# Attention scores on TensorE: base rows of two heads on different halves of the partitions

## What is computed

```python
q, k, v = heads(x @ Wq.T), heads(x @ Wk.T), heads(x @ Wv.T)      # 16 heads of 16
scores = einsum('bhid,bhjd->bhij', q, k) / sqrt(hd)
std_out = out_proj(softmax(where(mask, scores, neg)))            # plain
qg, qd = splat_feats(q)                                          # exp(-distance), tanh(direction)
kg, kd = splat_feats(k)
splat_attn = einsum('bhin,bhjn->bhij', amp * qg, kg) \
    + directional_strength * einsum('bhin,bhjn->bhij', amp * qg * qd, kg * kd)
gsa_out = out_proj(softmax(where(mask, scores + position_sensitivity * splat_attn, neg)))   # guided
attn = (1.0 - blend) * std_out + blend * gsa_out
x = layernorm(x + attn)
h = silu(x @ w_gate) * (x @ w_up)
x = layernorm(x + keep_2_largest_of_4(h) @ w_down)
```

## Time and profile before

| | us |
|---|---|
| median of 3 runs | 396.21 |
| lowest, highest run | 395.86, 396.52 |
| span of the profiled execution | 396.0 |
| PE busy in it | 372.8 (94%) |
| DVE busy | 303.9 (77%) |
| ACT busy | 229.6 (58%) |
| POOL busy | 125.7 (32%) |

### The profile page before, as it was taken

How to read it: one execution, slowest core, us unless ns; L and a number is a source line. 1 busy time by engine, 2 the same in 40 slices (tenths; PEclk the granted TensorE clock), 3 DMA queues, 4 the chain that set the end, 5 groups by cost and what they waited for, 6 DMA issues and landing times.

```text
span 396.0 us, 6714 instructions
## 1 busy us (share of the span) xinstructions
PE 372.8 (94%) x2234; PEld 255.1 (64%) x2234; DVE 303.9 (77%) x900; ACT 229.6 (58%) x451; POOL 125.7 (32%) x173
## 2 busy tenths in 40 slices
PE   6998999999999999999999999999889899999995
PEld 6666568565665665675664664764435488888884
DVE  2766999997897897897898898795024367999955
ACT  3965443675675685684784774775766836443100
POOL 8377657403303303302302312284395200000000
PEclk9998999999999999999999999999989999999999
DMA  6062540450540540540550558000000000000003
GB/s 201 22 105 47 81 81 4 67 95 10 88 70 4 87 75 6 89 73 4 82 82 3 80 86 319 4 2 0 5 0 2 0 2 0 0 2 0 2 0 106
DMA packets 12907, 19.70 MB, mean 50 GB/s; under 512 B 5492, under 2 KB 8564, under 8 KB 12872
## 3 DMA queue, kind: packets, MB, share of 16 engines
q1 hardware_dynamic: 10328, 18.18, 22.9%
q0 software_dynamic: 1536, 1.07, 1.6%
q10 hardware_dynamic: 1008, 0.02, 0.1%
HBM read 5.26 MB, written 1.05 MB: 16 GB/s over the span
## 4 chain that ended last, share of the span: by engine, by line
PE 69%; DVE 19%; ACT 6%; issue 2%; DMA 2%; SPq 1%; POOL 0%; DVEq 0%; ACTq 0%
PE ps L937 17%; PE ps L963 14%; PE ps L902 13%; DVE ps L1270 11%; PE ps L863 7%; PE ps L765 5%; PE ps L767 5%; PE ps L766 5%; DVE mpart L1263 2%; PE ps L924 2%; ACT pr L713 2%; DMA x_sb<-_attn_hidden_states_dram 2%; DVE mpart L1270 2%; PE ps L847 1%; PE ps L827 1%
## 5 line engine op out<-in xcount | busy, mean ns | idle before, releaser
L713 ACT ACTIVATE pr<-ps 128x512 f32<-128x512 f32 (+2 forms) x320 | 154.8, 571 | 75.8 <-PE ps L963 74.7
L1270 DVE CUSTOM_DVE_ANT_0 ps<-ps,causal 128x512 f32<-128x512 f32 (+3 forms) x256 | 144.9, 615 | 19.0 <-PE ps L902 18.2
L902 PE MATMUL ps<-k_st,q_st 65*128 65x512 f32 (+5 forms) x384 | 120.9, 369 | 3.5 <-DVE mpart L1270 2.8
L963 PE MATMUL ps<-q_st,k_st 67*128 67x512 f32 (+7 forms) x384 | 122.2, 363 | 0.3 <-ACT pr L713 0.3
L963 PEld LDWEIGHTS ps<-q_st,k_st 67*128 67x128 f32 (+1 forms) x384 | 68.3, 191 | 39.4 <-issue 21.5
L902 PEld LDWEIGHTS ps<-k_st,q_st 115*128 115x128 f32 (+1 forms) x384 | 67.9, 190 | 25.8 <-DVE mpart L1270 15.7
L937 PE MATMUL ps<-pr,vx 128*32 128x512 f32 (+3 forms) x768 | 74.1, 497 | 1.9 <-ACT o_sb L699 1.0
L558 POOL TENSOR_SCALAR_AFFINE_SELECT pr<-pr 128x512 f32<-128x512 f32 x64 | 40.5, 634 | 87.7 <-ACT pr L713 87.3
L1263 DVE TENSOR_REDUCE mpart<-ps 128x1 f32<-128x384 f32 (+2 forms) x96 | 54.9, 596 | 7.3 <-PE ps L902 7.0
L937 PEld LDWEIGHTS ps<-pr,vx 128*32 128x32 f32 x768 | 19.4, 109 | 32.1 <-issue 17.4
L1270 DVE DVE_READ_ACCUMULATOR2_ANT mpart<- 128x1 f32 x256 | 36.0, 141 | 0.0
(11 more groups left out here) (190 smaller groups left out, 497.5 us busy)
## 6 DMA issues: line engine op xcount, KB each, us to landing
q_st<-base_hiq SPq DMA_DIRECT2D x28, 64.0 KB
k_st<-base_hik SPq DMA_DIRECT2D x28, 64.0 KB
q_st<-feat_hiq SPq DMA_DIRECT2D x28, 64.0 KB
k_st<-feat_hik SPq DMA_DIRECT2D x28, 64.0 KB
x_sb<-_attn_hidden_states_dram SPq DMA_DIRECT2D x4, 256.0 KB, 6.5
raw<-in_L_ffn_w_gate_dram SPq DMA_DIRECT2D x1, 1024.0 KB, 4.8
raw<-in_L_ffn_w_up_dram SPq DMA_DIRECT2D x1, 1024.0 KB, 7.0
wd<-in_L_ffn_w_down_dram SPq DMA_DIRECT2D x1, 1024.0 KB, 9.1
```

Source lines behind the costliest of these rows:

```text
L713: act.activation(pr[:, s % NP, 2 * hh + vs[0]:2 * hh + vs[-1] + 1, d:BANK], src, ACT.Exp, scale=SCALE).then_inc(exp_done, 1)
L902: mm = pe.matmul(ps[:, slot, at:at + n], q_st[b][0:rows, hh, i * P:(i + 1) * P], k_st[b][0:rows, hh, first:first + n], start=(v == v0), st ...
L963: mm = pe.matmul(ps[:, bank, j * width:(j + 1) * width], k_st[b][0:rows, hh, kt * P:(kt + 1) * P], q_st[b][0:rows, hh, q:q + width], start ...
L1270: ins = dve.tensor_tensor_reduce(out=ps[:, slot, at:at + n], in0=ps[:, slot, at:at + n], in1=causal[:, BANK - n:BANK], scale=1.0, scalar=- ...
```

## The change

Head 0 keeps its base rows on partitions 0 to 47 and puts its feature rows on 64 to 111. Head 1 has them the other way round: features on 0 to 47, base on 64 to 111. In each half two rows behind them hold maxima. So the plain matmuls of head 0 use partitions 0 to 63 and those of head 1 use 64 to 127, 64 rows each, and the guided ones of both use all 128. k's stack is all ones before its rows are filled, q's all zeros.

The plain matmuls of the two heads stand one behind the other: `score_parts` has the heads innermost, `row_items` too from pair 1 on, and `leads` marks a maxima item whose partner of head 1 is taken with it. Nothing is put between the first two parts of a wide step. `rows` on DVE makes three operations of two, since each half of the partitions has its own order of plain and difference, and SP clears two pairs of rows instead of one when a buffer is used again.

```diff
-    BASE, FEAT = 0, 67
-    M_ROW, D_ROW = 65, FEAT + 3 * SPL
-    ZERO = 3 * HD
-    PLAIN, GUIDED = M_ROW, D_ROW
+    HROWS = P // KC
+    M_OFF = 3 * HD
+    Z_OFF = M_OFF + 2
+    BOTH = slice(0, P)
+    def own_rows(hh):
+        return slice(HROWS * hh, HROWS * hh + HROWS)
+    def base_row(hh):
+        return HROWS * hh
+    def feat_row(hh):
+        return HROWS * (1 - hh)
...
-        return [(hh, v, d, w) for hh in range(2) for v in ([(0, 1)] if w <= HALF else [(0,), (1,)])]
+        return [(hh, v, d, w) for v in ([(0, 1)] if w <= HALF else [(0,), (1,)]) for hh in range(2)]
...
+        return [("max", p, hh, i, c, v, nv) for i in range(T)
+                for c, piece in enumerate(row_pieces(i)) for v, nv in banks(piece) for hh in range(KC)]
+    def leads(it):
+        return it[0] == "max" and it[1] > 0 and it[2] == 0 and it[5:] == (0, 1)
...
+            for _ in range(2 if leads(stream[sent]) else 1):
+                here.append(stream[sent])
+                run_m += cost_m[sent]
+                sent += 1
...
-                        sp.dma_start(q_st[b][M_ROW:M_ROW + 2, hh, :].bitcast(F32),
-                                     k_st[b][ZERO:ZERO + 2, hh, :].bitcast(F32)).then_inc(st_loaded[b][hh], 16)
+                        for first in (0, HROWS):
+                            sp.dma_start(q_st[b][first + M_OFF:first + M_OFF + 2, hh, :].bitcast(F32),
+                                         q_st[b][first + Z_OFF:first + Z_OFF + 2, hh, :].bitcast(F32)).then_inc(st_loaded[b][hh], 16)
...
-                for n, (tile, rows, value) in enumerate(((q_st[b], slice(0, 128), 0.0), (k_st[b], slice(0, 64), 0.0),
-                                                         (k_st[b], slice(64, 128), 1.0))):
-                    pool.memset(tile[rows].bitcast(F32), value).then_inc(reused[b], 1)
+                for n, (tile, value) in enumerate(((q_st[b], 0.0), (k_st[b], 1.0))):
+                    pool.memset(tile[:].bitcast(F32), value).then_inc(reused[b], 1)
...
-                        rows = (PLAIN, GUIDED)[v]
-                        mm = pe.matmul(ps[:, slot, at:at + n], q_st[b][0:rows, hh, i * P:(i + 1) * P],
-                                       k_st[b][0:rows, hh, first:first + n], start=(v == v0), stop=True,
+                        rows = (own_rows(hh), BOTH)[v]
+                        mm = pe.matmul(ps[:, slot, at:at + n], q_st[b][rows, hh, i * P:(i + 1) * P],
+                                       k_st[b][rows, hh, first:first + n], start=(v == v0), stop=True,
...
-                    q, rows = g * BANK + d, (PLAIN + 2, GUIDED + 2)[v]
+                    q, rows = g * BANK + d, (own_rows(hh), BOTH)[v]
...
                 for t in range(len(parts[s])):
                     scores(s, t)
+                    if t == 0 and parts[s][0][1] == (0,):
+                        continue
                     for _ in range(4 // len(parts[s])):
                         if mine and mine[0][0] != "yt":
+                            together = leads(mine[0])
                             item(mine.pop(0))
+                            if together:
+                                item(mine.pop(0))
...
-                    dve.tensor_scalar(mdiff[:, 0], plain, -1.0, None, ALU.mult)
-                    link(dve.tensor_tensor(mdiff[:, 1], plain, guided, ALU.subtract))
+                    dve.tensor_scalar(mdiff[:].rearrange("p a h t -> p (a h) t")[:, 0:4:3], plain, -1.0, None, ALU.mult)
+                    for hh in range(KC):
+                        ins = dve.tensor_tensor(mdiff[:, 1 - hh, hh], plain[:, hh], guided[:, hh], ALU.subtract)
+                    link(ins)
```

More of the change, by code:

```diff
@@ L84, in row_items, with banks @@
     def row_items(p):
-        groups = [range(TPG * g, TPG * (g + 1)) for g in range(G)] if p == 0 else [range(T)]
-        return [("max", p, hh, i, c, v, nv) for tiles in groups for hh in range(KC) for i in tiles
-                for c, piece in enumerate(row_pieces(i))
-                for v, nv in (((0, 2),) if max(piece[1], HALF) <= HALF else ((0, 1), (1, 1)))]
+        def banks(piece):
+            return ((0, 2),) if max(piece[1], HALF) <= HALF else ((0, 1), (1, 1))
+        if p == 0:
+            return [("max", p, hh, i, c, v, nv) for g in range(G) for hh in range(KC) for i in range(TPG * g, TPG * (g + 1))
+                    for c, piece in enumerate(row_pieces(i)) for v, nv in banks(piece)]
+        return [("max", p, hh, i, c, v, nv) for i in range(T)
+                for c, piece in enumerate(row_pieces(i)) for v, nv in banks(piece) for hh in range(KC)]
+    def leads(it):
+        return it[0] == "max" and it[1] > 0 and it[2] == 0 and it[5:] == (0, 1)
     per_pair = len(row_items(0))
@@ L153, in build_kernel @@
         while sent < len(stream) and run_m - m_start < run_t * total_m / total_t:
-            here.append(stream[sent])
-            run_m += cost_m[sent]
-            sent += 1
+            for _ in range(2 if leads(stream[sent]) else 1):
+                here.append(stream[sent])
+                run_m += cost_m[sent]
+                sent += 1
             if sent % per_pair == 0:
@@ L356, in loads @@
         def loads(b, count):
-            return 16 * (13 * (count - 1) if b == 0 else 12 * count + (count - 1))
+            return 16 * (14 * (count - 1) if b == 0 else 12 * count + 2 * (count - 1))
         A_ACT, A_DVE = counted(A_USES, A_READ, "a"), counted(A_USES, A_READ, "d")
@@ L390, in first_base @@
         def first_base(queue, w, hf):
-            queue.wait_ge(reused[0], 3)
+            queue.wait_ge(reused[0], 2)
             queue.wait_ge(a_act, A_ACT[a_index[("proj", 0, w, hf)] + 1])
@@ L439, in _ @@
             for p in range(1, NB):
-                sp.wait_ge(reused[p], 3)
+                sp.wait_ge(reused[p], 2)
                 whole(p)
@@ L563, in maxima @@
                 pool.wait_ge(ring_free, ring_at[("turn_max", p)] + 1)
-                for row, first in ((M_ROW, 0), (D_ROW, 32)):
+                for row, first in ((M_OFF, 0), (HROWS + M_OFF, 32)):
                     pool.dma_start(q_st[p % NB][row:row + 2, :, :].bitcast(F32),
@@ L961, in scores @@
                 for j, v in enumerate(vs):
-                    q, rows = g * BANK + d, (PLAIN + 2, GUIDED + 2)[v]
-                    mm = pe.matmul(ps[:, bank, j * width:(j + 1) * width], k_st[b][0:rows, hh, kt * P:(kt + 1) * P],
-                                   q_st[b][0:rows, hh, q:q + width], start=(j == 0), stop=True,
+                    q, rows = g * BANK + d, (own_rows(hh), BOTH)[v]
+                    mm = pe.matmul(ps[:, bank, j * width:(j + 1) * width], k_st[b][rows, hh, kt * P:(kt + 1) * P],
+                                   q_st[b][rows, hh, q:q + width], start=(j == 0), stop=True,
                                    skip_group_check=(j > 0))
```

11 lines of the change are left out of this document (6 added, 5 removed).

## The result

| | before | after |
|---|---|---|
| median of 4 runs, us | 396.07 | 461.48 |
| lowest, highest run | 395.86, 396.52 | 457.01, 469.12 |
| span of the profiled execution | 396.0 | 456.9 |
| mean granted clock of TensorE in it | 0.991 | 0.927 |

The changed kernel takes 1.157 times the time of the kernel before (95% interval 1.153 to 1.161). The direction was forecast; the size was not: 65 us were added to the median (62 by 457.95) where 31 were foreseen, and both 461 and 458 lie above the range of 393 to 450.

What follows compares the result with a forecast made beforehand. PE was taken as first limit, VectorE close behind. In seven pairs 59.5 us of shape changes less 24.5 of concurrency and 8 of absorbed waits gave +27; with opening +3 and last pair +1, 396.0 became 427 us, range 393 to 450.

Steps and rivals of the forecast that it cites:

- What bounds the kernel: Middle pair of about 30.4 us: PE holds 78% of the chain of waits, DVE about 20%.
- The price of a change of shape: On PE, from gaps around probability-times-value matmuls: 0.19 us a change, 313 more changes in seven pairs, 59.5 us.
- Free shape changes: Rival: weights load ahead, PE falls to 25.1 us a pair and DVE becomes the bound; 379 us, chance 0.18.
- a change of shape costs about 0.1: Rival: 31 us of changes less 24.5, waits take most; 393 to 412, centre 399 us, chance 0.12.
- Concurrency: Adjacent plain matmuls of both heads run wholly side by side on PE: 3.5 us saved a pair, 24.5 over seven.
- The waits: PE's waits for DVE, 1.8 us a pair, 12.6 in all; a slower PE absorbs two thirds, 8 us.
- The third small operation: In VectorE's rows step, 0.18 us once a pair: hidden where PE is late, otherwise 1.4 us in all.
- The sum at full clock: 396.0 us plus 27 in seven pairs, 3 in the opening and 1 in the last pair: 427 us.
- the last sentence on the clock: TensorE's granted clock should stay at 2.4 GHz, as it does before in 38 of 40 slices.

Runs made afterwards that it cites:

- the chains: No attention computed: loops of matmuls on fixed data, one after another, run once; 64 and 128 rows in turn at 512 columns start 0.427 us apart.
- the first filler: Changed kernel with the plain 256-wide maxima of the first two row tiles issued three times instead of once: 450.77 us, ratio 1.135 to the kernel before.
- the regrouped kernel: Changed kernel's layout with all 64-row matmuls of a step first, 296 changes of shape instead of 497: 404.69 us, ratio 1.022 to the kernel before.
- the second filler: Kernel of the first filler with the plain 64-row matmuls of the narrow scores issued three times too: 465.62 us, ratio 1.175 to the kernel before.

## Why the prediction was right in part and wrong in its number

**What bounds the kernel** was read rightly: PE first, VectorE close behind.

**The price of a change of shape**, 0.19 us, worked out from the two edges of a value block, held: 0.20 at 512 columns alone, 0.18 at 256, 0.15 to 0.18 at 128. Four matmuls of 256 columns, forecast at 1.2 us, were measured at 1.25. Of the 373 changes between 64 and 128 rows in the changed kernel, 2 have a weight load that starts ahead of its matmul; among full-height matmuls it is 834 of 858. "Free shape changes" and "a change of shape costs about 0.1" are out.

**Concurrency** held too, 0.003 us apart in the chains. But not every couple is one: of the 123 adjacent plain couples of 384 and 512 columns 95 started within 0.03 us of each other in the changed kernel; nearly all of the rest found the second bank still with ScalarE or VectorE. "I take the full gain" was too much: 24.5, where the 86 couples that ran together in the seven pairs make about 19 by the prediction's own prices, and the kernel with both heads on one half lost only 13.5 in these pairs.

**The waits.** "I take two thirds, 8" of 12.6 us of VectorE waits as absorbed left out that the new order costs time of its own: 1.1 to 1.5 us a pair at full clock, 9.3 in all, as the run of the order on the old layout showed. The forecasts that PE would hold over 90% of the chain and VectorE below 10% were wrong where the clock is full (76% and 24%). The third small operation, put at "0.18 us", was named, but that one of these operations would meet the mask and take 0.62 was not; in the changed kernel it does in all seven pairs.

**The sum at full clock** came out nonetheless: five of the seven pairs at 34.2 to 34.4 us where 34 was forecast, +28.5 in seven pairs for +27, +1.6 in the last for +1, +1.1 in the opening for +3 (the opening before lost 1.7 to a low stretch that after does not have, so nearer to 3 than it looks). That is +31 in total, as forecast, but in part by luck, with terms that offset each other: fewer couples and more waits against cheaper changes in the narrow parts. How they split exactly the runs don't say. Two readings were off without harm: the row taken for the last pair (271 to 300) holds 8.8 us of the seventh, as the last one runs from 279.8 to 309.7, and 0.10 for a 128-wide matmul is a mean that takes in 256-wide ones.

**The step that failed** is the last sentence on the clock: "The granted clock should stay at its upper level, 2.4 GHz". It had no term in the sum and no rival. I took the clock from how busy PE was, and it would get busier. The runs show that the busy share is no guide to it: the chains in turn at 256 columns ran at half clock with PE busy 34.00 of 34.00 us, and in four pairs the changed kernel's clock fell behind six such maxima in a row. The 30.7 us lost in the seven pairs make up the difference between 427 and the profiled 456.9. That a thin stream can bring the clock down is shown by the chains. That it is what does it in the kernel is supported by the first filler, which took away the 13.65 us stretches and 7.2 us of time, and by the regrouped kernel, whose seven pairs stay at full clock; against it stand the second filler and the two places with the same six maxima and no fall. What starts each single stretch stays open.

## What to carry to other kernels

Before splitting the array's rows to run two matmuls at once, count the changes of shape in the order of the stream: each cost 0.15 to 0.20 us here, nearly the 0.23 that a couple of 512 columns saves, so a couple between full-height matmuls lost (1.087 us for the four against 0.908), and a couple is one only if both output banks are free at that moment. A change that spreads the same columns over more time on TensorE needs a term for the clock in its forecast, whatever the busy share says; here it was worth as much as all the rest. Price a new order by itself, on the old layout, before what it is for: here it alone cost 4%.

## What the runs showed of the hardware

- Two 64-row matmuls on different halves, 512 columns each, start 0.003 us apart and take 0.226 us together, the 0.227 of one full-height matmul; both weight loads start together too.
- 64 and 128 rows in turn: 0.427 us each at 512 columns, 0.312 at 256, 0.254 at 128 with the clock at 2.4 GHz; 0.510 at 256 and 0.403 at 128 at 1.2 GHz.
- A chain of full-height 256-wide matmuls that wait for their own end (0.442 us each) went to 1.2 GHz (0.640 each), with waits of 0.26 us between them and no change of shape.
- A subtraction on VectorE of 128x8 values took 0.16 to 0.17 us by itself and 0.62 us when it met GpSimd's mask; a conversion of 128x32 values took 0.18 and 0.62.
